# A graph layer with linear attention, masked attention and 32 experts on one core: edge keys turned once and compared beside the weight splits, the tail of attention woven with the output projection, a reordered routing, and an index column copied one step earlier

## The reference

```python
def _build_mask(edge_index, edge_type, edge_type_weights, dtype):
    src, dst = (edge_index[0], edge_index[1])
    w = jax.nn.softplus(edge_type_weights)
    mask = jnp.full((N, N), -jnp.inf, dtype=dtype)
    mask = mask.at[src, dst].set(w[edge_type - 1])
    diag = jnp.diagonal(mask)
    idx = jnp.arange(N)
    mask = mask.at[idx, idx].set(jnp.where(jnp.isneginf(diag), w[3], diag))
    return mask
...
q = x @ wq.T + bq; k = x @ wk.T + bk; v = x @ wv.T + bv
# q2, k2, v2: a second projection of each, cut into 16 heads of 64
scores = jnp.einsum('hnd,hmd->hnm', q2, k2) * scale + mask[None]
attn = jax.nn.softmax(scores, axis=-1)
out = jnp.einsum('hnm,hmd->hnd', attn, v2)   # then @ wo.T + bo
...
qf = jax.nn.elu(q) + 1.0; kf = jax.nn.elu(k) + 1.0      # linear attention, 16 heads
out = q_kv / denom                                       # then @ wo.T + bo
...
# x = x + gnn(xn) + mix(xn), xn = layernorm(x); then x + ffn(layernorm(x)):
gates = sigmoid(xt @ expert_sel.T); the four largest of 32 experts per token
out = sum over them of (relu(xt @ keys[e]) * gate) @ values[e]
```

## Time and profile before

| | us |
|---|---|
| median of 3 runs (range) | 960.46 (959.93 to 962.93) |
| profiled execution, its time | 962.8 |
| profiled execution, its span | 960.6 |
| PE busy in the span | 887.3 (92%) |
| DVE / ACT / POOL busy | 663.0 / 530.2 / 335.1 |
| mean granted clock of PE, share of full | 0.966 |

### The profile page before, as it was taken

The page is one execution under the profiler, slowest core; times in us unless marked ns, Lnnn a source line. Parts: engine busy times, 40 slices in busy tenths (PEclk is TensorE's granted clock), DMA queues, the critical chain, the costliest instruction groups (busy, mean ns, idle before and its releaser), DMA issues.

```text
span 960.6 us, 13957 instructions
## 1 busy us (share of the span) xinstructions
PE 887.3 (92%) x4482; PEld 749.9 (78%) x4482; DVE 663.0 (69%) x1050; ACT 530.2 (55%) x686; POOL 335.1 (35%) x292
## 2 busy tenths in 40 slices
PE   2789999999999999898984899999999999999993
PEld 2788889988989999644774788878888888888882
DVE  6676766653343544567387599979888899988880
ACT  3244421242322422467232388878888888888870
POOL 0703444454442000299101113433334344443331
PEclk9999999999999999999995699999999999999997
DMA  7423332223335333200282499999999999999941
GB/s 305 167 88 138 132 132 89 88 90 131 132 133 181 118 109 124 88 1 1 88 321 117 161 327 362 363 319 355 358 362 367 365 364 366 364 358 365 365 138 21
DMA packets 40453, 203.00 MB, mean 211 GB/s; under 512 B 12880, under 2 KB 13136, under 8 KB 18400
## 3 DMA queue, kind: packets, MB, share of 16 engines
q1 hardware_dynamic: 26496, 186.66, 51.8%
q0 software_dynamic: 13200, 15.03, 6.4%
q10 hardware_dynamic: 720, 0.83, 0.2%
HBM read 203.33 MB, written 21.15 MB: 234 GB/s over the span
## 4 chain that ended last, share of the span: by engine, by line
PE 67%; DMA 13%; POOL 7%; DVE 7%; issue 2%; ACT 2%; ACTq 0%; POOLq 0%; DVEq 0%; SPq 0%
PE ps L1103 20%; PE ps L1105 20%; PE ps L1104 20%; POOL pr L389 6%; DMA out_dram<-ysb,pcol 3%; DMA xg<-xt_dram,gcol 2%; DMA raw_x<-in_values 2%; DMA raw_x<-in_keys 2%; DMA out_dram<-etmp,pcol 2%; PE ps L1286 2%; PE ps L1133 1%; PE ps L1217 1%; PE ps L1292 1%; DMA c_all<-in_c_all 1%; POOL out_dram L574 1%
## 5 line engine op out<-in xcount | busy, mean ns | idle before, releaser
L632 ACT ACTIVATE wh<-raw 128x1024 fp32r<-128x1024 f32 x88 | 93.1, 1061 | 253.0 <-PE ps L1105 242.2
L788 DVE TENSOR_TENSOR wl<-raw,wh 128x1024 fp32r<-128x1024 f32 x88 | 110.7, 1263 | 156.8 <-ACT wh L632 156.4
L547 POOL DMA_INDIRECT plane<-code,idx x96 | 101.1, 1053 | 124.0 <-DMA plane<-code,idx 86.3
L1103 PE MATMUL ps<-wh_x,hTh 128*128 128x512 f32 x248 | 103.3, 416 | 0.0
L1103 PE MATMUL ps<-wh,xgTh 128*128 128x512 f32 x248 | 98.2, 396 | 0.0
L1105 PE MATMUL ps<-wh_x,hTl 128*128 128x512 f32 x248 | 98.2, 396 | 0.0
L1104 PE MATMUL ps<-wl,xgTh 128*128 128x512 f32 x248 | 97.9, 395 | 0.0
L1105 PE MATMUL ps<-wh,xgTl 128*128 128x512 f32 x248 | 97.8, 394 | 0.0
L1104 PE MATMUL ps<-wl_x,hTh 128*128 128x512 f32 x248 | 97.6, 393 | 0.0
L389 POOL TENSOR_SCALAR pr<-pr,mx 128x384 f32<-128x384 f32 x48 | 58.7, 1238 | 100.9 <-DVE mx L358 100.9
L1103 PE MATMUL ps<-xnh,wh 128*128 128x384 f32 x256 | 87.5, 342 | 2.7 <-issue 2.7
(11 more groups left out here) (221 smaller groups left out, 2031.2 us busy)
## 6 DMA issues: line engine op xcount, KB each, us to landing
raw<-in_keys SPq DMA_DIRECT2D x34, 1024.0 KB, 11.4
raw_x<-in_values SPq DMA_DIRECT2D x34, 1024.0 KB, 12.3
raw_x<-in_keys SPq DMA_DIRECT2D x30, 1024.0 KB, 12.2
raw<-in_values SPq DMA_DIRECT2D x30, 1024.0 KB, 12.5
raw<-in_w_v SPq DMA_DIRECT2D x8, 1024.0 KB, 4.8
raw<-in_w_q SPq DMA_DIRECT2D x8, 1024.0 KB, 4.9
raw<-in_w_k SPq DMA_DIRECT2D x8, 1024.0 KB, 4.8
raw<-in_w_mq SPq DMA_DIRECT2D x4, 1024.0 KB, 7.8
```

What stands on the lines that cost most here:

```text
L547: nc.gpsimd.indirect_dma_start(plane[m], bass.IndirectOffsetOnAxis(idx[:, g:g + 1].bitcast(U32), 0), code[:, g:g + 1], None, bounds_check= ...
L632: nc.scalar.activation(wh[:, s % SUB], raw[:, c % RAW, 2 * (s % 2):2 * (s % 2) + 2, :], ACT.Copy)\
L788: nc.vector.tensor_tensor(wl[:, s % SUB], raw[:, (s // 2) % RAW, 2 * (s % 2):2 * (s % 2) + 2, :], wh[:, s % SUB].bitcast(F32), ALU.subtrac ...
L1103: nc.tensor.matmul(o, ah, bh_, start=start, stop=False)
```

## The change

**Opening.** The identity is loaded alone and first, SP starts the weights when the second block of x has landed, and the other constants come behind x. DVE makes the keys between the first and second blocks' statistics. PE turns all keys at once (96 x 128), ACT copies them (`key_t`), GpSimd writes them to DRAM (`key_dram`) and reads them back as rows broadcast to all partitions, six loads of 16 groups each, into three buffers `key_rows`, in memory that `v` takes later. DVE compares from these buffers, four compares behind each weight split (`same_keys`), and there are no `dup` jobs. The empty planes are written from one tile by six DMAs, and three indirect writes set the diagonal. One of the biases is added to the other first, so there are four additions and not six; they stand behind the fourth broadcast. The x transposes use all eight banks.

**Attention.** The first four units' scores are made ahead of the last quarter of k21. ACT normalizes every sixth unit. Values come behind the turns of their step, and o0's products are put between the last turns and values. The splits that o0 still lacks are made in step 8, and four splits of the expert stage at the end of attention, where before they were made between o0 and o1 on DVE.

**Routing.** Other banks for turns, logits and ranks; the copy of `xtT` stands ahead of the first choice; `slot1h_h` and `lane1h` are made in three parts by ACT; `slot1h` follows `gidx` directly; the first slot's x is split in two halves and two half chunks of keys precede the second slot's turn; splits 6 and 7 come behind the second slot's x.

**Expert loop.** GpSimd waits for the result, issues the scatter-add, then the gather, copies the next slot's index column into the other of two `pcol` buffers, and waits for the landing.

The core of the diff:

```diff
-    names = ["xT0", "xT1", "mq0", "dup0", "mq1", "dup1", "mk0", "dup2", "mk1", "dup3", "mv0", "dup4",
-             "mv1", "dup5", "lin", "v0", "mix0", "mix1", "mix2", "v1", "mT0", "mT1", "mo0", "mo1",
+    names = ["xT0", "xT1", "mq0", "mq1", "mk0", "mk1", "mv0", "mv1", "lin", "v0", "mix0", "mix1", "mix2", "v1", "mT0", "mT1", "mo0", "mo1",
...
+EARLY = 4
+SPLIT_STEP = 8
+AHEAD = 4
...
+                if 0 <= i - 1 < STEPS and normed_by_act(2 * i - 1):
+                    normed(2 * i - 1)
+                if i == SPLIT_STEP:
+                    split_out()
+                if i - 4 == STEPS - 1:
+                    act.wait_ge(s_t, 2 * STEPS)
+                    split_ahead()
...
+            for i in range(STEPS + 3):
+                if EARLY // 2 <= i < STEPS:
+                    scores(pe, i)
+                if i == 3:
+                    pe.wait_ge(s_free, att_free + EARLY)
+                if i >= 3:
                     turn(2 * (i - 3))
                     turn(2 * (i - 3) + 1)
+                if i == STEPS:
+                    values_of(PAIRS - 2)
+                if i < STEPS and i >= 4 and (i - 4) % NT == NT - 1:
+                    values_of((i - 4) // NT)
+                if i == STEPS:
+                    out_part(0, 1)
+                if i == STEPS + 1:
+                    out_part(1, 2)
+            out_part(2, 4)
+            values_of(PAIRS - 1)
+            out_part(4, DC)
...
-            sp.wait_ge(s_const, 16 * N_CONST)
+            sp.wait_ge(s_x[NT - 2], 16)
...
+            def rows_of_keys(k):
+
+                g = GROUP * GROUPS[k]
+                pool.dma_start(key_rows[k % 3][:, :], key_dram[g * P:(g + GROUP) * P, :].rearrange("e o -> o e").to_broadcast([P, GROUP * P]))\
+                    .then_inc(s_rowk[k % 3], 16)
+
+            pool.wait_ge(s_keyc, 1)
+            pool.dma_start(key_dram.rearrange("(g p) o -> g (p o)", p=P), key_t[0:EC, :]).then_inc(s_keyd, 16)
+            pool.wait_ge(s_keyd, 16)
+            for k in range(3):
+                rows_of_keys(k)
+            pool.wait_ge(s_none, 1)
+            for m in range(2):
+                for t in range(NT):
+                    pool.dma_start(plane_rows[m][:, t, :], none[:, :]).then_inc(s_init, 16)
+            pool.wait_ge(s_idx, 1)
+            rows_of_keys(3)
...
             def pool_slot(j, p, count, ahead):
                 s = 2 * j + p
-                nc.gpsimd.tensor_copy(pcol[:, :], gidx[:, bass.ds(s, 1)]).then_inc(s_pch, 1)
-                pool_wait(s_pch, count + 1)
                 pool_wait(s_ye, s + 3)
-
-                nc.gpsimd.indirect_dma_start(out, bass.IndirectOffsetOnAxis(pcol[:, :].bitcast(U32), 0), ysb[p], None,
+                pool_wait(s_pch, count)
+
+                nc.gpsimd.indirect_dma_start(out, bass.IndirectOffsetOnAxis(pcol[p][:, :].bitcast(U32), 0), ysb[p], None,
                                              bounds_check=N - 1, oob_is_err=False, compute_op=ALU.add).then_inc(s_sc, 16)
                 if ahead:
                     pool_wait(s_xT, s + 3)
-                    gather(s + 4, p, count + 2)
+                    gather(s + 4, p, count + 1)
+                nc.gpsimd.tensor_copy(pcol[1 - p][:, :], gidx[:, bass.ds(s + 1, 1)]).then_inc(s_pch, 1)
                 pool_wait(s_sc, 16 * s + 16)
                 pool.sem_inc(s_scd, 1)
...
+                        if name == "v0" and b == 0:
+                            act.wait_ge(s_idx, len(GROUPS))
...
+            act.wait_ge(s_token, 1)
+            act.wait_ge(s_in, 1)
+            for t in range(NT):
+                nc.scalar.activation(slot1h_h[:, t, :, :], inslot_h[:, t, :, :], ACT.Copy, scale=token[:, t:t + 1]).then_inc(s_1s, 1)
+            for t in range(NT):
+                act.wait_ge(s_1h, t + 1)
+                ks = slice(t * TOPK, (t + 1) * TOPK)
+                nc.scalar.activation(lane1h[:, ks, :], lane1h_h[:, ks, :], ACT.Copy).then_inc(s_lane, 1)
...
-            x_hi(1, 0)
+            act.wait_ge(s_xT, 1)
+            nc.scalar.activation(xgTh[0][:, 0:4, :], x_banks[:, 0:4, :], ACT.Copy).then_inc(s_x0h, 1)
+            nc.scalar.activation(xgTh[0][:, 4:8, :], x_banks[:, 4:8, :], ACT.Copy).then_inc(s_xhi, 1)
...
+            def same_keys(u):
+
+                k, c = u // 4, u % 4
+                if c == 0:
+                    dve.wait_ge(s_rowk[k % 3], 16 * (k // 3 + 1))
+                for q in range(4 * c, 4 * c + 4):
+                    g = GROUP * GROUPS[k] + q
+                    link(nc.vector.scalar_tensor_tensor(junk[:, :], key_rows[k % 3][:, q * P:(q + 1) * P], ef[:, 3, g:g + 1],
+                                                        after[:, :], ALU.is_equal, ALU.mult, accum_out=dup[:, g:g + 1]))
...
+                    if s >= jobs["mq1"]["sub_end"]:
+                        for u in range(units[0], min(units[0] + (2 if s == jobs["mk0"]["sub_end"] else 1), 4 * len(GROUPS))):
+                            same_keys(u)
+                            units[0] += 1
...
-                    empty_planes(link)
+                if name == "k21":
+
+                    split(j["sub_end"] + LEAD - 1)
+                    for u in range(EARLY):
+                        masked(dve, u)
...
-                    link(nc.vector.tensor_scalar(token_h, cst["own"][:, NT:2 * NT], NOBODY - FAR, None, ALU.add))
-                    for k in range(4):
-                        split_expert(k, 0)
+                    nc.vector.tensor_scalar(token, cst["own"][:, NT:2 * NT], NOBODY - FAR, None, ALU.add).then_inc(s_token, 1)
...
-            choose(0)
             dve.wait_ge(s_xtt, 2 * NT)
             nc.vector.tensor_copy(xtT[:, 4:8, 2 * P:3 * P], ps[turn_banks[2][1]][:, :].rearrange("p (c t) -> p c t", t=P)).then_inc(s_xtc_dve, 1)
+            choose(0)
...
+            nc.vector.tensor_tensor(slot1h[:, :, :, :], inslot_h[:, :, :, :], four(m8[:, :, 0:TOPK, None], SLOTS), ALU.mult).then_inc(s_gate, 1)
...
-            for k in range(6, 8):
-                split_expert(k, 0)
-            x_lo(1, 0)
+            dve.wait_ge(s_x0h, 1)
+            nc.vector.tensor_tensor(xgTl[0][:, 0:4, :], x_banks[:, 0:4, :], xgTh[0][:, 0:4, :].bitcast(F32), ALU.subtract).then_inc(s_x0l, 1)
+            dve.wait_ge(s_xhi, 1)
+            nc.vector.tensor_tensor(xgTl[0][:, 4:8, :], x_banks[:, 4:8, :], xgTh[0][:, 4:8, :].bitcast(F32), ALU.subtract).then_inc(s_xlo, 1)
+            dve.wait_ge(s_r, NT + 4)
+            nc.vector.tensor_copy(tabf[:, :], ps[6][:, 0:SLOTS]).then_inc(s_gate, 1)
             x_lo(2, 1)
-            for k in range(8, 10):
+            for k in range(6, 10):
...
+                    pe.wait_ge(s_key, 1)
+                    nc.tensor.transpose(ps[0][0:EC, 0:P], ef[:, 3, :], ident).then_inc(s_keyt, 1)
+                    pe.wait_ge(s_keyc, 1)
+                    for t in range(NT):
+                        pe.wait_ge(s_xn, t + 1)
+                        for o in range(DC):
+                            last = nc.tensor.transpose(ps[o][:, t * P:(t + 1) * P], xn[:, t, o * P:(o + 1) * P], ident)
+                            if t == NT - 1:
+                                last.then_inc(s_bank, 1)
...
-                if name.startswith("dup"):
-                    pe.wait_ge(s_key, 1)
-                    for b in range(4):
-                        for q in range(4):
-                            g = GROUP * GROUPS[half] + 4 * b + q
-                            last = nc.tensor.transpose(bk[b][:, q * P:(q + 1) * P], ef[:, 3, g:g + 1].to_broadcast([P, P]), ident[:, :])
-                        last.then_inc(s_bank, 1)
...
+                        if name == "k21" and q == 3:
+                            for i in range(EARLY // 2):
+                                scores(pe, i)
...
             x_T(0, 16)
-            do_keys(0, 0, 0, 1, range(0, 1))
+            pe.wait_ge(s_x0l, 1)
+            for q in range(2):
+                half_chunk(q, 0, (xgTh[0], xgTl[0]), q, ps[0][:, :], q == 0, False)
+            pe.wait_ge(s_xlo, 1)
             x_T(1, 16)
-            do_keys(0, 0, 0, 1, range(1, 4))
+            do_keys(0, 0, 0, 1, range(2, 4))
```

309 lines of the change are left out of this document (178 added, 131 removed).

## The result

The changed kernel takes 929.75 us (median of 4 runs, 928.84 to 931.19) against 960.81 for the kernel before beside it: a ratio of 0.9675, interval 0.9654 to 0.9696. Predicted were 919.0 us; the gain is 31.1 us and not 41.5. The profiled execution has a span of 926.1 us, 34.5 less than before. Three executions further down, one without the early units and two with the first choice ahead, were slow ones of 1098 us and more, and no median or ratio here holds them.

What follows compares the result with a forecast made beforehand. PE was taken to pace all but routing, with DMA close in the expert stage. Opening 23.6, attention 7.5, routing 10.0 and expert stage 0.4 sum to 41.5 us: 960.46 to 919.0 us, range 910 to 931 for 8 in 10.

Steps and rivals of the forecast that it cites:

- the two waits: Opening: PE's waits of 4.93 us for the keys and 4.32 us for mq, 9.25 us, were to go.
- a rival 4 us: Opening: GpSimd's bias additions hold DVE, two splits at 3.1 instead of 1.2 us where PE waits; 923 us, 12%.
- the lost cover: Opening: the last group of keys had covered DVE's three copies of mv, so `lin` will wait 0.9 us for the last.
- The estimate of 25: Opening: about 25 us for one 1 MB broadcast of keys, from the 512 KB biv_b row at 13.6 us.
- under 1: Attention: the sign that PE's idle time there falls under 1 us, from 8.05 us in the window.
- loads pile up until ACT waits for them, whatever PE does before: Expert stage: why ending PE's 2.5 us of waits for gathered rows isn't a gain of 2.5; 0.4 us was taken.
- The rival that loads don't bind (15%): Expert stage: PE's stall and about 1.5 us of clock behind it are gained too; 915 us, 15%.
- the index copy misses its aim: Expert stage: the landing spaces GpSimd's rounds, PE's 2.5 us of waits stay; 919 to 921 us, counted in the base.
- The 0.7 us at the very end: End of the expert stage: the index copy and a short wait are off the path, 0.7 us gained.
- the sign named for the loads: Expert stage: ACT's waits for raw in the last 50 us stay as long or longer, behind a DMA share of 1.00.
- 10 us to spare: Opening: slack seen for GpSimd's 96 indirect writes before DVE reads the mask in k1; a start 18 us late costs 8.
- That rival's 927 us: Opening into k1: the scatters end late, GpSimd's 96 indirect writes finishing after DVE needs the mask; 927 us, 6%.

## Why the prediction was right or wrong

**Opening: 19.6 instead of 23.6.** The 96 transposes and the two waits went. (The group listed with 1.91 us is the one of 1.75 from start to start, so the transposes are 12.4 us and not 12.5, which changes nothing.) Four terms of the sum were off. The first product came 1.8 us earlier, not 2.4. The bias additions, to which the sum gave zero and a rival 4 us, cost 1.4: the hold was on four short operations around the codes, 7.3 us of VectorE's time, and not on splits, as the earlier trace rows had shown it; the run without the additions shows it. For `lin` the prediction named the lost cover and put it at 0.9 us; it was 1.9, because by the order four compares stand between the last split and the copies of mv, and in six of the eleven profiles the clock fell in the products behind it, 1.64 us more. Moving the compares brought it to 0.88. mal and mixed waited 1.9 us against 1.5. These add up to 5.0; about 1 us came back, since the first products of mq no longer start at half clock (0.45 us listed for the first, 0.66 in the earlier trace rows; the granted clock was 0.68 from 21.5 to 26 us before and is 1.00 from 19.7 to 24 now), which the sum hadn't counted.

**The broadcasts** were no danger: 5.0 to 11.8 us to landing, half of them under 6. The estimate of 25, twice the 13.6 of the half-size row, scaled the wrong row: biv_b itself took 13.2 us again, and what makes that row load slower than a broadcast of twice its size wasn't tried.

**Attention: 7.6 instead of 7.5.** GpSimd's group is at 40 units and PE sets the pace; PE's idle time is 1.8 us where "under 1" had been forecast. The prediction left out that the early scores lengthen k21 by 1.5 us. It put GpSimd's pace 0.2 us over PE's for each three steps, 1.6 in all, and taking GpSimd off the pace was worth 3.5 us: the sum, which was taken from the idle time as a whole, came out better than its parts.

**Routing: 10.0 as summed**, with one sign wrong inside: the copy of xtT ahead of the first choice costs 1.1 us at full clock and was counted among the gains. The last choice was released 13.4 us behind o1's end and not 20.2: 6.7, against 6.1. That errors of both signs cancel to 10.0 is luck.

**Expert stage: -2.65 instead of 0.4.** The step that failed is "loads pile up until ACT waits for them, whatever PE does before". It was read from one row, 22.02 us for the last load, and from a DMA share of 1.00. With an eighth of the bytes of the loop taken away the loads of values landed in 6.5 us, and the stage was no shorter. The rival that loads don't bind (15%) was the right one, and its gain appears only in the kernel with the two splits, whose expert stage is 3.3 us shorter than before in one pair of profiles (over all of them the two ranges overlap). What took its place in the changed kernel was the late place of splits 6 and 7: the prediction saw that they free buffers 3 us later, and not that they leave VectorE without a gap when GpSimd's first scatter-add is due. That the index copy misses its aim was named too; the landing doesn't space the rounds, PE's result does. The 0.7 us at the very end didn't come either: from the start of the last `ysb` to the last scatter-add it takes 9.3 us before and 9.4 now. And the sign named for the loads decides nothing: ScalarE's waits for raw in the last 50 us are 4.2 us before, 4.4 in the changed kernel's first profile and none in its second.

**The scatters of edges** ended later than the prediction's 10 us to spare allow, and VectorE waited for them in k1, up to 6.5 us, with no wait of PE behind it. That rival's 927 us is the nearest to the measured time, but not by its cause.

**The median.** The forecast took the sum from a median of 960.46. The profile says 34.5, the medians 31.1. Two places where the clock went one way or the other in the profiles, `lin` and the last logits, 1.6 us each, can be part of the spread of 3.3 us in the spans of the changed kernel's four runs (926.1 to 929.4); only one of the four has a trace.

## What to carry to other kernels

Where two engines hold each other up at SBUF, as VectorE and GpSimd do here, ask at each place where one of them issues something short and urgent whether the other is behind with its work: 5 us of hold came from 2.4 us of work that had been moved out of an idle time. A DMA share of 1.00 with a long time to landing said here that loads were queued, not that they were late; only a run with fewer bytes, or a wait on PE's own path, tells. And work taken off an engine that doesn't set the pace there was worth nothing: the index copy was moved, and the time was the same.

## What the runs showed of the hardware

The issue of an indirect scatter-add by GpSimd took 1.6 us at the least, 2.2 to 2.6 beside splits of VectorE that wait for ScalarE, and 6.7 to 6.9 beside splits that follow one another directly. How short a gap is enough isn't resolved. The Trainium skill (SBUF — State Buffer, "Who interferes with whom") states that the pair of ports that VectorE and GpSimd share is an exclusive lock; for the additions the trace agrees: the held code operations took 2.3 to 2.4 us each, as long as one of the additions (7.17 us for three). For the scatter-add the section points the other way: TENSOR_TENSOR takes only the pair's read side, and the making of descriptors needs the write side, which it calls inferred. The runs decide: moving two splits took the issue from 6.7 to 2.6 us, and a waiting GpSimd was passed over by four splits that started one behind the other. By the same section the compares, with two operands in SBUF, would be held by the additions: 2.49 instead of 0.35 us, so the trace agrees. TENSOR_SCALAR with one tensor operand was held as well, 2.31 instead of 0.27 us; the section counts it among the operations that can take both pairs, where their operands allow it.

After a wait of 1.9 us the granted clock in the same 48 products was full in some executions of the same order, and 0.83 on the mean from 122 to 132 us in others: the products took 5.60 or 7.24 us.
